# A delta-rule attention and mixture-of-experts kernel: decays by a scan, whole-width levels, a bank pair for each stage, an order table per engine

## The reference

```python
mixed = silu(_causal_conv(hidden_states @ w_qkv, conv_w))        # 4 taps
beta = sigmoid(b);  g = -exp(A_log) * softplus(a + dt_bias)
def step(state, xs):
    q_t, k_t, v_t, g_t, b_t = xs
    state = state * jnp.exp(g_t)[..., None, None]
    kv = jnp.einsum('bhk,bhkv->bhv', k_t, state)
    delta = (v_t - kv) * b_t[..., None]
    state = state + jnp.einsum('bhk,bhv->bhkv', k_t, delta)
    out = jnp.einsum('bhk,bhkv->bhv', q_t, state)
    return (state, out)
o = o * silu(z);  o = o * rsqrt(mean(o * o) + EPS) * norm_gamma;  return o @ w_out
```

## Time and profile before

| what | value |
|---|---|
| median of 3 runs | 2755.87 us (2755.43 to 2758.89) |
| the profiled execution's own time | 2757.2 us |
| its span, first to last instruction | 2755.4 us |
| mean granted TensorE clock | 0.993 of full |
| TensorE busy | 2551.5 us, 93% |
| its weight loads | 1941.1 us, 70% |
| VectorE busy | 2210.7 us, 80% |
| ScalarE busy | 1648.0 us, 60% |
| GpSimd busy | 1199.9 us, 44% |
| moved by DMA | 31.17 MB |

### The profile page before, as it was taken

The page is one execution under the profiler, slowest core; times in us unless marked ns, Lnnn a source line. Parts: engine busy times, 40 slices in busy tenths (PEclk is TensorE's granted clock), DMA queues, the critical chain, the costliest instruction groups (busy, mean ns, idle before and its releaser), DMA issues.

```text
span 2755.4 us, 56912 instructions
## 1 busy us (share of the span) xinstructions
PE 2551.5 (93%) x21606; PEld 1941.1 (70%) x21606; DVE 2210.7 (80%) x4991; ACT 1648.0 (60%) x4887; POOL 1199.9 (44%) x1003
## 2 busy tenths in 40 slices
PE   5999999999999999999999999999999999998998
PEld 4777777777777777777777777777777777776665
DVE  4888888888888888888888888888888888886665
ACT  3666666666666666666666766666666666664110
POOL 3445444454445544454445544454445544452000
PEclk9999999999999999999999999999999999998999
DMA  1000000000000000000000000000000000001000
GB/s 60 2 17 1 17 1 1 17 1 17 1 17 2 17 1 2 16 1 17 1 17 2 17 1 2 17 1 17 1 16 2 17 1 1 17 2 68 16 16 16
DMA packets 12909, 31.17 MB, mean 11 GB/s; under 512 B 2400, under 2 KB 7008, under 8 KB 12384
## 3 DMA queue, kind: packets, MB, share of 16 engines
q1 hardware_dynamic: 12640, 27.54, 2.9%
HBM read 25.44 MB, written 2.10 MB: 10 GB/s over the span
## 4 chain that ended last, share of the span: by engine, by line
PE 73%; ACT 15%; DVE 7%; issue 4%; POOL 0%; DMA 0%; SPq 0%; POOLq 0%; DVEq 0%; ACTq 0%
PE bank L839 16%; PE bank L1020 9%; PE bank L863 6%; ACT og L1077 5%; PE bank L929 4%; PE bank L982 4%; PE bank L482 3%; PE bank L912 3%; PE bank L1003 3%; PE bank L969 3%; ACT L1081 3%; PE bank L992 3%; ACT dec L1081 3%; ACT X L1084 2%; PE bank L1011 2%
## 5 line engine op out<-in xcount | busy, mean ns | idle before, releaser
L1137 DVE SCALAR_TENSOR_TENSOR conv<-bank,cw_all,conv 128x511 f32<-128x511 f32 (+2 forms) x768 | 554.4, 743 | 12.3 <-ACT conv L1051 3.1
L749 POOL TENSOR_TENSOR decb<-dec,sc_all 128x512 f32<-128x512 f32 x128 | 130.4, 1039 | 883.6 <-ACT dec L1081 883.6
L839 PE MATMUL bank<-xT,w_kh 128*128 128x512 f32 x1024 | 498.9, 600 | 0.7 <-ACT sc_all L372 0.7
L1051 ACT ACTIVATE conv<-bank,cw_all 128x512 f32<-128x512 f32 x256 | 176.1, 688 | 454.9 <-PE bank L839 454.9
L1186 DVE TENSOR_TENSOR N<-bank,lev 128x256 f16<-128x256 f32 x768 | 323.5, 421 | 125.2 <-PE bank L912 119.3
L1090 ACT ACTIVATE X<-bank 128x256 f16<-128x256 f32 x768 | 291.3, 379 | 166.1 <-PE bank L929 149.2
L929 PE MATMUL bank<-N,XT 128*128 128x64 f16 x3072 | 215.3, 192 | 73.5 <-DVE N L1186 58.1
L1020 PE MATMUL bank<-wo,ogT 128*128 128x256 f32 x1024 | 282.6, 399 | 0.0
L863 PE MATMUL bank<-w_kh,xT 128*128 128x256 f32 x1024 | 279.1, 395 | 0.0
L912 PE MATMUL bank<-X,mhiT 128*128 128x64 f16 x3072 | 219.0, 194 | 45.2 <-ACT X L1090 30.2
L780 POOL TENSOR_TENSOR ms<-ms,expo 128x8 f32<-128x8 f32 x64 | 105.3, 1645 | 332.7 <-DVE ms L1244 332.7
(11 more groups left out here) (164 smaller groups left out, 6210.4 us busy)
## 6 DMA issues: line engine op xcount, KB each, us to landing
w_kh<-w_heads SPq DMA_DIRECT2D x16, 768.0 KB, 4.3
wo_raw<-w_out SPq DMA_DIRECT2D x16, 256.0 KB, 4.6
xT<-x_cols SPq DMA_DIRECT2D x4, 512.0 KB, 8.3
zone<-x_rows SPq DMA_DIRECT2D x4, 512.0 KB, 3.7
xT<-gate_up SPq DMA_DIRECT2D x1, 2048.0 KB, 8.7
out<-og SPq DMA_DIRECT2D x4, 512.0 KB, 2.9
conv<-down SPq DMA_DIRECT2D x1, 1024.0 KB, 9.7
tri_sb<-tri SPq DMA_DIRECT2D x1, 256.0 KB, 2.7
```

Of the source, the lines that this page charges most:

```text
L839: mm = pe.matmul(FB[g][:, :], w_kh[:, k, g * P:(g + 1) * P], xT[:, k, (b % B) * SEQ:(b % B + 1) * SEQ], start=(k == 0), stop=(k == KT - 1))
L1137: dve.scalar_tensor_tensor(conv[:, g, j:], FB[g][:, 0:SEQ - j], cw_all[:, head, g * TAPS + 3 - j:g * TAPS + 4 - j], conv[:, g, j:], op0=AL ...
```

## The change

Per body, five things are different; the experts are the same but for the buffers they use and for where their preparation is put.

- **Decays by a scan.** The exps of g and of its running sum are taken once for all bodies, transposed to rows and written to a DRAM buffer `rows`. For each body the sync engine reads them back, spread over the partitions, as `egb` and `ecb` (512 KB each, two buffers each). GpSimd writes a diagonal of beta over the key's square norm into decb (`diag`), and two `tensor_tensor_scan` of 128x512 on VectorE (`scan`) run state = egb * state + decb along the tokens. The seg products, mask, products L848 and L850, exp and its table load, and the product by beta are gone. `m` and `p` are now plain products of 128x512.
- **q with its decay.** GpSimd makes qE = q * ecb, and `out` adds qE times S and pT times U in one bank; recall, recalled and the adding in gated are gone. `og` is one product of 128x512 per half.
- **Keys** are copied from PSUM by ScalarE (`kraw`) and scaled on GpSimd.
- **Whole-width levels.** Every join, growx and growt takes all 8 cells (8 products of 64 columns in one bank), and N, X and XT are written by one instruction of 128x512 each, XT always on ScalarE. **Banks:** P0 and P1 for projections, transposes and gate, I0 and I1 for products, levels, newton and finish, R0 and R1 for the recurrence, O0 and O1 for out, turn and project.
- **Order.** One table per engine. Each entry has `ahead` 0 or 1: in turn k it belongs to body k or k + 1. Steps of level 0 to 3, and join and growx of level 4, stand at the end of a turn for body k + 1; growt of level 4, level 5, newton and finish stand in the next turn, now as body k, between the first projections of the following body.

```diff
-            pe.matmul(dst[:, :], identb[:, :], negm[:, :], start=True, stop=False, skip_group_check=True)
-            for part in range(2):
-                mm = pe.matmul(dst[:, :], after_r[:, :], gseg[:, part, 4 * i:4 * i + 4, :], start=False,
-                               stop=(part == 1), skip_group_check=True)
-            act.activation(half(dec, i), bank4((B2, B3)[i]), ACT.Exp).then_inc(s_dec, 1)
+            d = half(decb, i).rearrange("p x t -> p (x t)")
+            dve.tensor_tensor_scan(d, egb[:, p, 512 * i:512 * i + 512], d, 0.0, ALU.mult, ALU.add).then_inc(s_scan, 1)
...
-            for x in range(4):
-                mm = pe.matmul(level_banks(i)[0][h][:, x * 64:(x + 1) * 64], mhiT[:, 4 * h + x, :],
+            for x in range(CELLS):
+                mm = pe.matmul(IB[1 - i % 2][:, x * 64:(x + 1) * 64], mhiT[:, x, :],
...
+            if c > 0:
+                pe.matmul(dst, qE[:, p, x, :], S[:, c, v * P:(v + 1) * P], start=True, stop=False)
+            mm = pe.matmul(dst, pT[:, p, x, :], U[:, x, :], start=(c == 0), stop=True)
...
+for n in range(BODIES):
+    for dst, i, s_load, s_free, m in ((egb, 0, s_eg, s_scan, 2), (ecb, 1, s_ec, s_qe, 1)):
+        if n > 1:
+            sp.wait_ge(s_free, m * (n - 1))
+        sp.dma_start(dst[:, n % 2], ...)
...
+ORDER = {"vector": [
+        ("join", 5, 0), ("conv", 0, 1), ("conv", 1, 1), ("conv", 2, 1), ("res", 0, 0), ("res", 1, 0), ("tt", 0, 0),
+        ("tt", 1, 0), ("norms", 0, 1), ("conv", 3, 1), ("conv", 4, 1), ("s", 0, 0), ("conv", 5, 1), ("scan", 0, 1),
+        ("rhs", 1, 0), ("scan", 1, 1), ("m", 0, 1), ("m", 1, 1), ("s", 1, 0), ("conv", 6, 1), ("p", 0, 1),
...
+        ("rhs", 3, 0), ("conv", 10, 1), ("og", 0, 0), ("p", 1, 1), ("conv", 11, 1), ("og", 1, 0), ("join", 0, 1),
+        ("factor", 0, 0), ("join", 1, 1), ("qnorm", 0, 1), ("join", 2, 1), ("join", 3, 1), ("join", 4, 1),
+        ("acc", 0, 0), ("acc", 1, 0),
```

More of the change, by code:

```diff
@@ L49 @@
 NX = NE + 1
[L50 to L74, removed]
@@ L77, in build_kernel, with rounds @@
+def rounds(order):
+    most = max(ahead for _, _, ahead in order)
+    for k in range(-most, BODIES):
+        for name, i, ahead in order:
+            if 0 <= k + ahead < BODIES:
+                yield name, i, k + ahead
 def build_kernel(nc, x_rows, x_cols, w_heads, w_ab, conv_w, dt_bias, a_log, gamma, w_out,
@@ L392, in wide @@
             return flat(t).rearrange("p (c n) -> p c n", n=n)
-        xg = zone[:, 0, 0:CH * D].rearrange("p (c n) -> p c n", n=D)
-        x1 = [wide(t) for t in (dec, decb)]
+        xg = wide(qT)
+        x1 = [egb[:, i].rearrange("p (c n) -> p c n", n=D) for i in range(2)]
         hrow = wide(m32T)
-        sqx = wide(og2)
+        sqx = wide(keys[:, 0])
         hT = [wide(t, SEQ) for t in (vT, rhs)]
@@ L400, in build_kernel @@
         aT = wide(U, SEQ)[:, 0:2]
-        y = wide(qs)
+        y = wide(qE[:, 0])
         outrow = wide(og)
@@ L425, in build_kernel @@
         }
[L426 to L427 removed]
+        PREPARE = {
+            "vector": {("og", 0): (0,), ("og", 1): (2, 4), ("factor", 0): (6,), ("acc", 1): (8, 10)},
+            "scalar": {("power", 1): (3,), ("turn", 1): (7,)},
+            "tensor": {("turn", 1): (7,), ("project", 3): (8, 12)},
+        }
         def moe_loads(sp):
[L431 to L432 removed]
+            sp.wait_ge(s_kq, 2 * BODIES)
+            sp.wait_ge(s_ktp, 2 * BODIES)
+            sp.wait_ge(s_qe, BODIES)
             sp.dma_start(xg, x_rows[0:SEQ, :].rearrange("(c p) n -> p c n", p=P)).then_inc(s_xg, 16)
+            sp.wait_ge(s_proj, 4 * BODIES)
             sp.wait_ge(s_silu, 4 * BODIES)
@@ new lines, in run @@
+            def run(name, i, n):
+                p, q, head, b = n % 2, n % 3, n // B, n % B
+                w = w_kh[:, head % 2]
+                later = n > 0
+                if name == "proj":
+                    j, k = divmod(i, KT)
+                    g = COLS_OF[j]
+                    if i == 0 and b == 0:
+                        pe.wait_ge(s_w, 16 * (head + 1))
+                    if k == 0:
+                        if j < 2 and later:
+                            pe.wait_ge(s_zs, 2 * (n - 1) + j + 1)
+                        if j == 2:
+                            pe.wait_ge(s_sq, 8 * n + 4)
+                            pe.wait_ge(s_kraw, n + 1)
+                        if j == 3:
+                            pe.wait_ge(s_sq, 8 * n + 8)
+                    mm = pe.matmul(PB[j % 2][:, :], w[:, k, g * P:(g + 1) * P], xT[:, k, b * SEQ:(b + 1) * SEQ],
```

945 lines of the change are left out of this document (476 added, 469 removed).

## The result

The changed kernel takes **2770.21 us** (median of 5 runs, 2769.75 to 2771.23) against 2755.87 us for the kernel before in the same comparison: a ratio of 1.0051, with a 95% interval of 1.0037 to 1.0066. It is slower by half a per cent, where 2712 us and faster were forecast. The profiled execution took 2771.23 us over a span of 2769.5.

The account below looks back on a forecast made before the run. The length of a turn, with no engine full, bounds the kernel: legs of 15.1 and 22.8 make 37.9 us against 38.70. Over 63 turns, 2757.2 - 50 + 6 = 2713, less 1.3: 2712 us, range 2640 to 2800.

Parts of the forecast that it names:

- sharing with GpSimd: VectorE leg: first scan runs beside GpSimd's qE and nk (power for k's norm factors), charged 0.15 us.
- the VectorE leg: First conv to next N0: 22.8 us against 19.56, with pairs (two products that start the levels) at 1.52.
- The rule I cited: SBUF interfaces shared by GpSimd and VectorE: both scans, having two SBUF inputs, would pay, sum 0.15 us higher.
- The level leg: N0 to the first conv, the chain of levels: 15.1 us against 19.13.
- the rival that had them meet more traffic: Levels: another 0.42 us on each of five whole-width levels, turn 40.0, 2845 us; chance 0.22.
- The scan's price: Each VectorE scan taken at 1.23 us, the 1024-column product; 2.3 for two with the overlap.
- The rival with the product's rate (2643): Scans on VectorE: 0.54 us less each, turn 36.8, 2643 us; chance 0.13.
- The ends: Start and end outside the loop: start zero, later preparation of the first expert group plus 6 us, from 0 to 12.
- TensorE as no limit of the changed kernel: TensorE's work per turn shrinks to some 35 of 37.9 us; its 1.36 us gain costed at nothing.
- the signs that would make the prediction wrong: A gap before the scans released by GpSimd or a DMA, or N waiting over 3 us for a join.
- GpSimd's results are used two us or more after they can be ready: GpSimd's diag, keys and qE (1.9 us each for diag and keys): never late, so costed at nothing.
- The rival by which VectorE's and TensorE's waits stay as before (2677): Whole turn: legs overlap better, just the 1.36 us of decay go, turn 37.3, 2677 us; chance 0.20.

Follow-up runs that it names:

- experiment 1: GpSimd's table reordered in the changed kernel, so that none of its products runs beside VectorE's scans and pairs (port cleared): 2666.79 us, ratio 0.9683.
- experiment 5: Kernel before the change, with GpSimd's two fills of m32T held back until VectorE's two pairs are done: 2742.65 us, ratio 0.9958.
- experiment 4: Changed kernel with nk put in front of qE on GpSimd, same work: 2782.62 us, ratio 1.0105.
- experiment 11: Kernel of experiment 1 with each scan replaced by a product of the same operands, running sum left out: 2666.60 us, ratio 0.9685.
- 3: Changed kernel with only the pairs freed: GpSimd's z scaling ahead of the diagonal, keys behind mlo: 2717.67 us, ratio 0.9869.
- 6: Changed kernel with the last tap of each of four conv groups on 4 columns instead of 509: 2748.06 us, ratio 0.9977.
- 7: Kernel of experiment 1 with the last conv taps shortened to 4 columns instead of 509: 2637.03 us, ratio 0.9573.
- experiment 8: Kernel of experiment 1 with VectorE's step s 2 put behind conv 8: 2647.50 us, ratio 0.9614.
- experiment 10: Kernel of experiment 8 with TensorE's transposes vtp 0 put in front of growx 0: 2647.05 us, ratio 0.9608.

## Why the prediction was wrong

**Which step failed.** The term "sharing with GpSimd" in the sum of the VectorE leg. It had two parts. The first scan was charged 0.15, taken from the mean of the old pairs, 838 ns, over that of og, 692; it paid 0.88. The pairs were taken over at 1.52 for two, counted from their start to that of the next instruction, as if their neighbours would stay; these changed from an mhi and a fill to zs and keys, and the pairs took 2.17 counted the same way (1223.63 less 1221.46). That is 0.73 + 0.65 = 1.38 a turn too little, where the leg came out 1.14 too long; the difference, 0.24, is that the rest of the leg was walked too long. The walk itself holds: cleared of the port, the leg in experiment 1 is 22.28 us, 21.72 without the new wait of 0.56, and the forecast's 22.0 + 0.65 with the pairs at 0.75 instead of 1.52 is 21.9.

**Why it was mis-sized.** I read the old pairs as work that is slowed by a share. They were waiting: 410 ns of work and the rest of a neighbour (experiment 5). A wait isn't a property of the waiting instruction, so it can't be carried over or averaged; its size is what is left of the other engine's instruction when this one arrives, between 0 and 1.9 us. Comparing 838 with og's 692 hid this further, since the pairs are 16-bit and alone take 410. The order tables already showed the neighbours: qE stood beside the first scan, keys beside the pairs. The bound I left out was the length of the neighbour; with it this term alone would have had a range of 0 to 3.8 us a turn, twice 1.9 for the first scan and the pairs, against a gain of 0.8: the sign of the change was open.

The rule I cited, by which the Trainium skill's "GPSIMD Engine Reference" (1. Specifications) would have both scans pay, was half right: in each of these kernels one scan pays or none, and which depends on what GpSimd is doing. The Trainium skill says more in "SBUF — State Buffer" (Who interferes with whom; Summary: rules for kernel authors): an instruction of VectorE with two SBUF inputs contends with one of GpSimd that reads SBUF, and the second to issue is blocked until the first has finished. The runs here agree in both directions: scan 1.21 to 2.09, 2.27, 2.61 and, with qE cut, 1.55; nk 1.02 to 1.94, qE 1.82 to 2.63. They differ in one point, and there the measurement decides: a scan issued 0.22 or 0.39 us before the end of nk isn't held (experiment 4, and the second scan of the changed kernel).

**What was right.**
- The level leg: 14.95 for 15.1, steps from N to N of 2.4 to 3.1 us (forecast 2.4 to 2.9), and the rival that had them meet more traffic didn't come.
- The scan's price: 1.21 for 1.23. The rival with the product's rate (2643) had both its halves wrong: the scan isn't that fast, and experiment 11 shows that in the cleared kernel it wouldn't matter.
- The ends: the start 2.1 us earlier and the end 3.6 later (2769.5 - 2507.6 = 261.9 for 258.3), plus 1.5 for the 6 taken, within 0 to 12.
- TensorE as no limit of the changed kernel: experiment 1 takes 1.64 us out of a turn with none of its work touched. But "behind that VectorE has no gap, and TensorE's work waits for it, not the reverse" holds only until part of the leg is freed; in experiments 1 and 3 0.56 us of waiting for TensorE appears, and in 6, 7 and 11 such waits take most of what VectorE gives.

**What else was not right.** Of the signs that would make the prediction wrong, N waiting over 3 us and a gap before the scans, neither came. The failure is in no gap at all but inside the busy time of two rows, and my list named it only as "the first of a pair longer if the port is shared". That GpSimd's results are used two us or more after they can be ready doesn't hold for diag: it ends at 1212.93, and the scan starts at 1213.69. And that 2770 lies inside the stated range is luck: the range reached so high for the rival in which the levels meet more traffic, and the level leg came out 0.15 shorter than walked.

**The account of the 14 us.** Against the forecast's 37.9 the turn is 1.0 longer: +0.73 first scan, +0.65 pairs, -0.24 the rest of the leg, -0.15 the levels; 63 us, less 4.5 at the ends (1.5 for 6), is the 58 us between 2712 and 2770. The rival by which VectorE's and TensorE's waits stay as before (2677) is what experiment 1 comes near to, but by another road, so this is no support for it.

**What stays open.** How long nk holds the port isn't shown. What bounds the cleared kernel in the end wasn't settled: of a turn of 36.92 TensorE is busy 34.51 in experiment 8, and filling its longest gap gave nothing (experiment 10). A version that combines the shortest with qE cut was not tried.

## What to carry to other kernels

When an instruction of VectorE gets two operands in SBUF (a scan, a product of two loaded tensors), look up on GpSimd's timeline what will run beside it, and bound its cost by the whole of that neighbour's length, not by a share. The order of an engine that is only half busy can then be worth more than the change itself: here the change is worth 2.8% at most (experiment 5) and came out 0.5% slower, and moving four GpSimd steps into VectorE's idle stretch or beside its PSUM work took 3.7% off, with no instruction added; cutting one long step in two, with nothing moved, gave 1.1%. And before counting what a freed microsecond brings, ask what is next behind it: here 0.3 to 0.5 us of the 2.1 freed arrived, and waits for TensorE and for the port took the rest.
